# Loading routed tiles in 32 by 32 blocks and turning them on VectorE instead of on TensorE

## The reference: what is computed

```python
def _expert_stack(x, W1, b1, W2, b2):
    h = gelu(jnp.einsum('btd,edf->ebtf', x, W1) + b1[:, None, None, :], approximate=False)
    return jnp.einsum('ebtf,efd->ebtd', h, W2) + b2[:, None, None, :]
shared_enc = _expert_stack(x, sW1, sb1, sW2, sb2).sum(0)
weights = softmax(x @ gW + gb, axis=-1)
topv, topi = jax.lax.top_k(weights, 3)                   # 3 of 15 experts
gated = (one_hot(topi, 15) * topv[..., None]).sum(axis=-2)
router_out = _expert_stack(x, rW1, rb1, rW2, rb2)        # 128 -> 256 -> 128, all float32
router_enc = jnp.einsum('ebtd,bte->btd', router_out, gated)
return shared_enc + router_enc + x
```

## Time and profile before

| | |
|---|---|
| median of three runs | 347.08 us |
| the profiled execution | 346.81 us |
| its span, first to last instruction | 345.0 us |
| loads of tiles | issued from 224.3 to 293.5 us |
| scatters of tiles | 231.0 to 310.7 us (starts of the first and the last) |
| POOL busy in the span | 212.8 us (62%) |
| PE busy in the span | 255.0 us (74%) |
| DVE busy in the span | 217.9 us (63%) |

### The profile page before, as it was taken

One profiled execution on the slowest core, in us unless ns is written; L12 is line 12 of the kernel. 1 busy time (PEld: TensorE's weight loads), 2 busy tenths in 40 slices (PEclk: granted clock), 3 DMA queues, 4 the chain that ended last, 5 costly groups with the idle time before them and its releaser, 6 DMA issues.

```text
span 345.0 us, 7056 instructions
## 1 busy us (share of the span) xinstructions
PE 255.0 (74%) x2319; PEld 190.2 (55%) x2319; DVE 217.9 (63%) x578; ACT 181.0 (52%) x393; POOL 212.8 (62%) x219
## 2 busy tenths in 40 slices
PE   3989986776696877745997999879999898800700
PEld 1866755564452434314684867579998887700200
DVE  4568997974999999893646246446676555300650
ACT  2579792434769485423636242138886757700060
POOL 4426676425249994247788777617777777771480
PEclk9999999865999999875799579969999999965655
DMA  7974010124000077000111115233443333215512
GB/s 225 408 162 93 4 32 0 34 63 122 2 2 0 2 231 298 3 0 25 54 39 49 55 51 142 80 77 96 122 120 108 103 108 94 71 53 159 223 53 68
DMA packets 38196, 31.32 MB, mean 91 GB/s; under 512 B 12960, under 2 KB 31408, under 8 KB 37776
## 3 DMA queue, kind: packets, MB, share of 16 engines
q1 hardware_dynamic: 32448, 21.08, 21.0%
q0 software_dynamic: 3520, 7.27, 6.2%
q10 hardware_dynamic: 2192, 2.52, 2.4%
HBM read 19.38 MB, written 11.47 MB: 89 GB/s over the span
## 4 chain that ended last, share of the span: by engine, by line
POOL 33%; PE 23%; DVE 17%; issue 15%; DMA 7%; ACT 3%; SPq 0%; ACTq 0%; POOLq 0%; DVEq 0%
POOL x_srt L1558 13%; POOL k_heads L1527 6%; POOL v_pairs L1521 5%; PE psum L794 5%; PE psum L785 5%; POOL y_tok L1581 4%; DVE prob_sums L1227 3%; DMA y_tok<-k_heads,y_rows 2%; PE psum L582 2%; PE psum L481 2%; DMA v_pairs<-y_tok 2%; DVE maxes L1221 2%; DMA k_heads<-x_srt 1%; POOL rstd L1600 1%; DVE turned_room L1124 1%
## 5 line engine op out<-in xcount | busy, mean ns | idle before, releaser
L1581 POOL DMA_INDIRECT y_tok<-k_heads,y_rows x62 | 61.3, 989 | 27.6 <-issue 14.9
L1558 POOL DMA_INDIRECT x_srt<-v_blocks,slot x48 | 46.7, 974 | 14.3 <-issue 14.3
L1035 ACT ACTIVATE k_heads<-psum,k_heads 128x128 f32<-128x128 f32 x124 | 38.7, 365 | 16.9 <-PE psum L785 14.0
L1527 POOL TENSOR_TENSOR k_heads<-k_heads,inv_sums 128x1024 f32<-128x1024 f32 x16 | 30.9, 1934 | 26.9 <-DVE inv_sums L1232 26.9
L794 PE MATMUL psum<-k_heads 128*128 128x128 f32 x248 | 41.0, 289 | 4.4 <-ACT k_heads L1035 3.7
L785 PE MATMUL psum<-k_heads 128*128 128x128 f32 x248 | 39.9, 285 | 0.0
L794 PEld LDWEIGHTS psum<-k_heads 128*128 128x128 f32 x248 | 33.4, 196 | 8.0 <-ACT k_heads L1035 7.7
L785 PEld LDWEIGHTS psum<-k_heads 128*128 128x128 f32 x248 | 34.3, 200 | 0.5 <-DVE k_heads L1440 0.2
L1440 DVE COPY k_heads<-psum 128x128 f32<-128x128 f32 x62 | 18.0, 291 | 25.8 <-PE psum L777 25.2
L1424 DVE COPY k_heads<-expert_w 128x514 f32 x62 | 28.4, 464 | 3.4 <-issue 2.9
L1043 ACT ACTIVATE k_heads<-psum,k_heads 128x128 f32<-128x128 f32 x62 | 22.8, 368 | 13.9 <-DMA y_tok<-k_heads,y_rows 13.2
(11 more groups left out here) (161 smaller groups left out, 567.8 us busy)
## 6 DMA issues: line engine op xcount, KB each, us to landing
expert_w<-e_w SPq DMA_DIRECT2D x1, 4369.0 KB, 15.7
k_heads<-x_srt SPq DMA_DIRECT2D x62, 65.0 KB, 1.8
x_srt<-pad SPq DMA_DIRECT2D x16, 65.0 KB
xT<-x_t SPq DMA_DIRECT2D x4, 256.0 KB, 6.8
x_rows<-x_n SPq DMA_DIRECT2D x1, 1024.0 KB, 9.8
ctxT_k<-ctx_k SPq DMA_DIRECT2D x1, 1024.0 KB, 11.9
ctxT_v<-ctx_v SPq DMA_DIRECT2D x1, 1024.0 KB, 13.8
v_scr<-v_rows SPq DMA_DIRECT2D x4, 256.0 KB, 5.9
```

The costliest lines, as they stand in the source:

```text
L1035: ins = act.activation(h_tile[:, t % 2, a, :], bank[2 + t % 2][:, P * a:P * a + P], ACT.Gelu, bias=stage[:, t % NS, EW - 2 + a:EW - 1 + a])
L1527: pool.tensor_tensor(probs2[:, p % 3, :].rearrange("p (t h) -> p t h", t=B), probs2[:, p % 3, :].rearrange("p (t h) -> p t h", t=B), inv_s ...
L1558: pool.indirect_dma_start(out=x_srt, out_offset=bass.IndirectOffsetOnAxis(ap=slot[:, n:n + 1], axis=0), in_=payloads[:, g, k, :], in_offse ...
L1581: pool.indirect_dma_start(out=y_tok, out_offset=bass.IndirectOffsetOnAxis(ap=y_rows[:, t:t + 1].bitcast(mybir.dt.uint32), axis=0), in_=y_t ...
```

## The change: what it does

The load of a tile is split in two. The first DMA brings the 128 features, cut into 32 x 32 blocks: on partition 32a + i, block b, it puts the features 32a to 32a + 31 of token 4i + b. The second brings the gate and the destination row, with partition 32b + i for token 4i + b. Both add to the same semaphore, which is therefore waited for at 32 per load. VectorE's transpose instruction turns each 32 x 32 block in its place, and with it `x_tileT` has features on partitions, its columns the tokens in the order 32b + i. PE's turn and DVE's copy out of PSUM go, with their semaphore, and PE's list is one round shorter.

```diff
@@ sync
-                sp.dma_start(x_tile[:, t % NB, :], x_srt[bass.ds(row_of[t % 4], P), :]).then_inc(s_x_tile[t % NB], 16)
+                rows = x_srt[bass.ds(row_of[t % 4], P), :]
+                sp.dma_start(x_tile[:, t % NB, 0:E].rearrange("p (b j) -> p b j", b=4),
+                             rows[:, 0:E].rearrange("t (a j) -> a t j", a=4)).then_inc(s_x_tile[t % NB], 16)
+                sp.dma_start(x_tile[:, t % NB, E:XW], rows[:, E:XW].rearrange("(i b) c -> b i c", b=4)).then_inc(s_x_tile[t % NB], 16)
@@ tensor
-            def tile_turned(t):
-                pe.wait_ge(s_x_tile[t % NB], 16 * (t // NB + 1))
-                if t >= 2:
-                    pe.wait_ge(s_x_tileT, t - 1)
-                pe.transpose(bank[t % 2][:, 0:P], x_tile[:, t % NB, 0:E], ident).then_inc(s_tile_turned, 1)
...
-            for i in range(NT + 2):
+            for i in range(NT + 1):
                 if i < NT:
-                    tile_turned(i)
-                if 1 <= i < NT + 1:
-                    tile_in(i - 1)
-                if i >= 2:
-                    tile_out(i - 2)
+                    tile_in(i)
+                if i >= 1:
+                    tile_out(i - 1)
@@ vector
                 for t in range(first, first + n):
-                    dve.wait_ge(s_x_tile[t % NB], 16 * (t // NB + 1))
+                    dve.wait_ge(s_x_tile[t % NB], 32 * (t // NB + 1))
...
-            def xinT_out(t):
-                dve.wait_ge(s_tile_turned, t + 1)
+            def tile_turned(t):
+                dve.wait_ge(s_x_tile[t % NB], 32 * (t // NB + 1))
                 if t >= 2:
                     dve.wait_ge(s_tile_psum, t - 1)
-                dve.tensor_copy(x_tileT[:, t % 2, :], bank[t % 2][:, 0:P]).then_inc(s_x_tileT, 1)
+                dve.transpose(x_tileT[:, t % 2, :], x_tile[:, t % NB, 0:E]).then_inc(s_x_tileT, 1)
...
-                xinT_out(t)
+                tile_turned(t)
```

More of the change, by code:

```diff
@@ L260, in build @@
         s_x_tile = [sem(f"s_x_tile{k}") for k in range(NB)]
-        s_tile_turned = sem("s_tile_turned")
         s_x_tileT = sem("s_x_tileT")
```

## The result

The changed kernel takes 406.34 us (median of four runs, 405.31 to 407.68) against 347.23 us for the kernel before (four runs, one more than behind the 347.08 above); the ratio is 1.170, with a 95% interval of 1.167 to 1.174. The profiled execution took 406.25 us, its span 404.4. The forecast was 399, and a range of 362 to 428.

The account below looks back on a forecast made before the run. POOL's scatters, about 1.3 us per tile, were taken to bound the kernel before. With 62 loads at 2.16 us on four engines, the last scatter moves from 310.70 to 363.2: 346.8 plus 52.5 is 399.3, said as 399; range 362 to 428.

Parts of the forecast that it names:

- POOL is the bound before, and what PE and DVE save is worth nothing: Tiles' stage: POOL's scatters set 1.307 us per tile; PE and DVE savings gain nothing, except at most 0.6 us in run-up.
- The cut into 4 shares: Tile loads: the source pattern's outermost count of 4 gives 4 shares, on the same 4 DMA engines at each tile.
- a tile on one of the four engines, 2.16 us: Tile loads: per engine 1.60 us features, 0.35 gates, 0.02 closing packets and 0.19 scatter, sum 2.16, above POOL's 1.31.
- the lowest price of the prediction (1.79): Tile loads, every price at its lowest: 1.60 us features plus 0.19 scatter per tile on each of four engines; 376 us.
- SP at 1.03 to 1.23 us per tile: SP's issues of a tile's two loads: 1.03 to 1.23 us, just under POOL's 1.26 if nothing blocks.
- Rival B: Tile loads over 16 engines, but SP's issues, perhaps 1.5 us per tile, are the bound: +12, 359 us; chance 0.05.
- The end: End of the tiles' stage: first load issued at 224.3, last tile lands at 359.7, last scatter at 363.2 us, +52.5.
- A mean DMA share of 0.3: Sign in the changed kernel's tiles' stage: low mean DMA share, about 0.3, since only four engines are full.
- loads that land far later than 1.8 us after their issue: Sign in the changed kernel's profile: tile loads land far later than 1.8 us after issue, about 2.2 us between loads.
- a low clock: Sign in the changed kernel's profile: PE's clock at its low level for most of the tiles' stage.
- The transposes: DVE's 128x128 transposes between SBUF places: about 0.25 us each, costing nothing because DVE stays under POOL.

Follow-up runs that it names:

- e4: Kernel before with its one row-wise load, but VectorE turning blocks in place instead of PE's turn and the PSUM copy; ratios 0.990 and 0.994 to the kernel before.
- e3: Changed kernel's two new loads, with PE's turn and the PSUM copy kept as in the kernel before; 420.0 us, ratio 1.093 to the kernel before.
- e5: Kernel before, with a tile's single load naming its rows as 4 x 32 instead of 128; ratios 1.040 and 1.048 to the kernel before.
- e1: Changed kernel, both loads given outermost count 128, same piece sizes; 385.5 and 379.9 us beside 382.2 and 384.2 for the kernel before.
- e2: Changed kernel, feature load bringing only tokens 0 to 63 (256 pieces); 395.5 and 397.4 us beside 382.2 and 384.2 for the kernel before.
- e6: Changed kernel, second transfer (gate and destination row) read with outermost count 128, features still on 4; 410.4 us, ratio 1.072 to the kernel before.

## Why the prediction was right, and where it was not

- **POOL is the bound before, and what PE and DVE save is worth nothing.** Supported: e4 is 1.0% and 0.6% below the kernel before (the second not clear of noise), in jobs where POOL is less of a bound than it was, and e3, with the turn kept, is as slow as the whole change.
- **The cut into 4 shares.** Right, the step on which all hung: 4 closing packets per transfer in the changed kernel and in e5, 16 in e1, and the loss that this chip showed in these jobs vanishes with 16. The Trainium skill's rule ("DMA: Bandwidth & Descriptors", section "Why a DMA increments its semaphore by 16 and not by 1") agrees with these counts.
- **The term that was mis-sized: a tile on one of the four engines, 2.16 us.** At 9.4 ns per packet, a tile takes 1.52 us, with 0.19 of scatter 1.71, less than even the lowest price of the prediction (1.79). The engines are not what holds the loop, and the nearness of 2.16 to the measured 2.26 was luck. Its two errors (a duration taken for a distance; SP's price left too low) offset each other.
- **SP at 1.03 to 1.23 us per tile.** This step failed. I priced both issues from transfers over 16 engines. Over 4 an issue takes 0.55 and not 0.33 to 0.38 us (e5, e2), and the one behind 128 pieces per engine is held to 0.93 to 1.04 (e6, the changed kernel). With its gaps and the table load, which was left out of the sum, SP needs 2.24, never waits for a buffer, and is the bound. Rival B had the right engine and tied it to the wrong case.
- **The end.** The last scatter was due at 363.2 and came at 370.4: the first load was issued 1.4 us later than before, and 62 x (2.256 - 2.16) = 6.0. The sum 399.3 missed the profiled 406.25 by the same 7 us.
- **What the profile was to show.** A mean DMA share of 0.3, loads that land far later than 1.8 us after their issue, and a low clock.

The windows (us, busy times, granted clock, DMA share, GB/s), against the earlier trace rows:

```profile
250.00:300.00 50.00, 28.02 (x165) 26.01 (x164) 14.66 (x49) 19.36 (x63) 20.81 (x22) 0.83 0.30 58
300.00:350.00 50.00, 34.62 (x183) 33.34 (x184) 15.47 (x51) 21.46 (x68) 22.53 (x23) 0.70 0.31 60
```

The share is 0.30 and 0.31, but it cannot tell full engines from engines that are idle a quarter of the time at 0.345, which is why it seemed to confirm the wrong step. The first tile's load is issued at 225.75 and its last piece moves at 228.8, 3.1 us later, and about as much (3.2) in the middle of the stage (issue at 302.75, pieces moving from 304.0 to 305.9): later than 1.8, but no queue piles up on the engines, which full engines would have shown. PE's clock was not low for most of the stage: it is granted at 0.83 and 0.70 in the mean, so over these 100 us at its low level (1.2 GHz) about half of the time. The transposes took 0.31 and not 0.25 us, hidden all the same.

The Trainium skill, same section, says that over k engines the issuing sequencer itself writes the remaining 16 - k counts of the semaphore. This fits the 0.2 us by which each issue over 4 engines is longer (0.55 against 0.33 to 0.38); no run here separates that write from other causes. How the hardware holds back the issue behind a long transfer, whether by room in a queue or otherwise, is open too. Shown is that it depends on the pieces per engine ahead of it, that it needs no older work on the engines (first tile), and that in four tiles it ended 0.3 to 0.4 us after those pieces began to move.

## What to carry to other kernels

Look at the outermost count of both sides of a transfer before its bytes: a pattern that starts with 4 ran on 4 of 16 engines here. Neither part did the harm alone: 128-byte pieces over 16 engines cost nothing measurable (e1), long pieces over 4 engines 4 to 5% (e5), and the small pieces over 4 engines, 128 on each, 8% in the same conditions and 59 us in the first measurement. Price a transfer from a trace on the issuing queue as well as on the engines, with its spread the same as the new one's, and take the distance between packets and not their duration. Where work is taken off an engine that is hidden behind another (PE and DVE behind POOL here), little or nothing can be won, and the new form loses as soon as its transfers take SP or the DMA engines more than POOL's 1.3 us per tile.

## What the runs showed of the hardware that I had not expected

- SP's issue of a transfer over 4 engines takes 0.55 us, over 16 engines 0.33 to 0.38, for 128 as for 512 pieces.
- Behind a transfer of 128 pieces on each of four engines, the next issue on the queue takes 0.93 us instead of 0.36 (16 engines), and 1.04 instead of 0.55 (4 engines). Behind 64 pieces per engine it is not held.
- The table load on the same queue takes 0.81 us behind a transfer over 4 engines (the changed kernel, e5) and 0.30 behind one over 16 (the kernel before, e1), in the median.
- The issue that is held ends 0.28 to 0.38 us after the pieces ahead of it begin to move (four tiles of the changed kernel), also when the engines had nothing older to do.
- One DMA engine, if the 4 shares are 4 engines, moves a 128-byte piece from DRAM every 9.4 ns, while each is recorded as 12 to 13 ns long: shares of busy time overstate what an engine has to do.
